# Integer softmax of a vision tower: the left-over part is made by GpSimd in three passes

## The reference

```python
def _int_exp(x_int, s, n=30):
    x0_int = jnp.floor(LN2 / s)
    x_int = jnp.maximum(x_int, n * x0_int)
    q = ste_floor(x_int / x0_int)
    r = x_int - x0_int * q
    exp_int, es = _int_polynomial(r, s)
    exp_int = jnp.maximum(ste_floor(exp_int * jnp.exp2(n - q)), 0.0)
    return (exp_int, es / 2.0 ** n)
```

## Time and profile before

| | us |
|---|---|
| median of 3 runs | 561.8 |
| lowest and highest run | 560.23, 562.18 |
| the profiled execution, whole | 560.4 |
| its span in the profile | 558.6 |
| busy in the span: TensorE | 419.3 |
| VectorE | 317.6 |
| ScalarE | 247.1 |
| GpSimd | 143.7 |

### The profile page before, as it was taken

How to read it: one execution, slowest core, us unless ns; L and a number is a source line. 1 busy time by engine, 2 the same in 40 slices (tenths; PEclk the granted TensorE clock), 3 DMA queues, 4 the chain that set the end, 5 groups by cost and what they waited for, 6 DMA issues and landing times.

```text
span 558.6 us, 9536 instructions
## 1 busy us (share of the span) xinstructions
PE 419.3 (75%) x3508; PEld 308.4 (55%) x3509; DVE 317.6 (57%) x867; ACT 247.1 (44%) x518; POOL 143.7 (26%) x169
## 2 busy tenths in 40 slices
PE   4777785468778999999889994632794235799997
PEld 3545562246568885666555793321442233589996
DVE  3858875489855421223311128669898975645642
ACT  4235543336656411222222212693396665385661
POOL 3644443069911240000000054008010001113410
PEclk9969987559999999999999998575556555599999
DMA  8921111096004222111101071000000000000002
GB/s 296 404 105 19 17 18 19 14 397 284 4 1 193 84 101 86 48 47 39 58 19 39 29 287 51 0 1 3 2 0 0 2 5 1 2 0 1 1 19 72
DMA packets 19793, 38.64 MB, mean 69 GB/s; under 512 B 2136, under 2 KB 16164, under 8 KB 18340
## 3 DMA queue, kind: packets, MB, share of 16 engines
q1 hardware_dynamic: 18788, 35.41, 18.3%
q0 software_dynamic: 960, 2.62, 1.4%
HBM read 29.77 MB, written 7.01 MB: 66 GB/s over the span
## 4 chain that ended last, share of the span: by engine, by line
PE 52%; DVE 24%; ACT 10%; issue 6%; POOL 6%; DMA 1%; SPq 0%; DVEq 0%; ACTq 0%
PE psum L1255 11%; PE psum L1262 6%; PE psum L1287 5%; PE psum L2337 4%; PE psum L1301 3%; PE psum L2370 3%; POOL ring L782 3%; POOL experts L787 2%; PE psum L610 2%; PE psum L2376 2%; PE psum L1279 1%; ACT experts L1663 1%; PE psum L2354 1%; DMA experts<-in_tern 1%; DVE ring L1939 1%
## 5 line engine op out<-in xcount | busy, mean ns | idle before, releaser
L1255 PE MATMUL psum<-experts,ring 128*128 x136 | 64.3, 596 | 1.9 <-issue 1.2
L1079 DVE TENSOR_TENSOR ring<-ring,psum 128x512 f32<-128x512 f32 x17 | 11.7, 688 | 62.8 <-PE psum L1255 62.8
L1186 POOL DMA_INDIRECT front<-expert_results,slot_of x10 | 9.9, 992 | 125.0 <-DMA expert_results<-ring 122.2
L1262 PE MATMUL psum<-front,shared 128*128 128x256 f32 (+1 forms) x160 | 34.6, 370 | 0.0
L1255 PEld LDWEIGHTS psum<-experts,ring 128*128 128x128 f32 x136 | 23.3, 190 | 19.4 <-issue 19.4
L1287 PE MATMUL psum<-experts,ring 128*128 x136 | 32.1, 379 | 0.0
L1287 PEld LDWEIGHTS psum<-experts,ring 128*128 128x128 f32 x136 | 25.8, 190 | 10.3 <-issue 7.6
L1262 PEld LDWEIGHTS psum<-front,shared 128*128 128x128 f32 x160 | 29.2, 190 | 3.2
L1385 ACT COPY ring<-psum 128x512 f32<-128x512 f32 x17 | 10.0, 586 | 42.3 <-PE psum L1279 42.3
L2337 PE MATMUL psum<-experts 128*128 128x256 f32 (+1 forms) x120 | 28.6, 384 | 0.0
L590 PE MATMUL psum<-experts,ring 128*128 128x256 f32 x108 | 25.9, 391 | 0.4 <-DVE experts L485 0.4
(11 more groups left out here) (364 smaller groups left out, 1076.0 us busy)
## 6 DMA issues: line engine op xcount, KB each, us to landing
experts<-in_experts SPq DMA_DIRECT2D x8, 1536.0 KB, 12.8
experts<-in_x SPq DMA_DIRECT2D x9, 384.0 KB, 8.2
expert_rows<-zeros SPq DMA_DIRECT2D x1, 2176.0 KB, 15.0
ring<-expert_rows SPq DMA_DIRECT2D x17, 128.0 KB, 2.1
shared<-in_shared SPq DMA_DIRECT2D x1, 1536.0 KB, 18.1
experts<-in_ffn_q SPq DMA_DIRECT2D x1, 1536.0 KB
experts<-in_ffn_s SPq DMA_DIRECT2D x1, 1536.0 KB
experts<-in_pos_embed SPq DMA_DIRECT2D x1, 1152.0 KB, 8.7
```

Of the source, the lines that this page charges most:

```text
L1079: nc.vector.tensor_tensor(o, o, up_bank(g), ALU.mult).then_inc(hidden_done.sem, 1)
L1255: mm = nc.tensor.matmul(bank, sl_xT[t % 2][:, k, :], slot_w(t, block, k, F), start=(k == 0), stop=(k == KD - 1))
L1262: mm = nc.tensor.matmul(o[:, b, 0:w], shared_w(block, k, (2 * half + b) * P, P), moe_x(c)[:, k, 0:w], start=(k == 0), stop=(k == KD - 1))
```

## The change

The pass left_over leaves VectorE. GpSimd does it in three passes: it copies `sm_d` to a new f32 buffer `sm_f` (two buffers, behind the others in `ring`), multiplies `sm_v` by minus x0 into `sm_r`, waits for that through a new semaphore count `sm_scaled`, and adds `sm_f`. The waits of left_over on exponential(t-3), whole(t) and shifted(t) go with it, and so does the signal `sm_left`, which ScalarE's whole and squared and VectorE's shifted wait for. The two memsets stand behind GpSimd's tile 4 instead of behind `k_root`, and clear only the half of each region that the V copies don't write.

```diff
+        sm_f = [view(ring, 4352 + u * N1, N1) for u in range(2)]
...
+        sm_scaled = Count("sm_scaled", pool_power, TOK)
...
-            def left_over(t):
-                dve.wait_ge(sm_whole.sem, sm_whole.done(t))
-                dve.wait_ge(sm_shifted.sem, sm_shifted.done(t))
-                if t >= 3:
-                    dve.wait_ge(sm_exp.sem, sm_exp.done(t - 3))
-                nc.vector.scalar_tensor_tensor(sm_r[t % 3], sm_v[t % 2], x0_neg, sm_d[t % 3], ALU.mult, ALU.add).then_inc(sm_left.sem, 1)
-
...
-                if 0 <= i - 1 < NT:
-                    left_over(i - 1)
...
-            pool.wait_ge(pv_vb_ready.sem, pv_vb_ready.done(0))
-            nc.gpsimd.memset(l1_f[:, 1, :], 0.0)
-            nc.gpsimd.memset(l1_f[:, 4, :], 0.0).then_inc(pv_zeroed.sem, 1)
+
+            def left_over(t):
+
+                pool.wait_ge(sm_shifted.sem, sm_shifted.done(t))
+                nc.gpsimd.tensor_scalar(sm_f[t % 2], sm_d[t % 3], 1.0, None, ALU.mult)
+                pool.wait_ge(sm_whole.sem, sm_whole.done(t))
+                if t >= 3:
+                    pool.wait_ge(sm_exp.sem, sm_exp.done(t - 3))
+                nc.gpsimd.tensor_scalar(sm_r[t % 3], sm_v[t % 2], x0_neg, None, ALU.mult).then_inc(sm_scaled.sem, 1)
+                pool.wait_ge(sm_scaled.sem, sm_scaled.done(t))
+                nc.gpsimd.tensor_tensor(sm_r[t % 3], sm_r[t % 3], sm_f[t % 2], ALU.add).then_inc(sm_left.sem, 1)
+
+            for t in range(NT):
+                left_over(t)
+                if t == 4:
+                    pool.wait_ge(pv_vb_ready.sem, pv_vb_ready.done(0))
+                    for a, i in enumerate((1, 4)):
+                        w = nc.gpsimd.memset(l1_f[:, i, :].rearrange("p (g a d) -> p g a d", a=2, d=HD // 2)[:, :, 1 - a, :], 0.0)
+                    w.then_inc(pv_zeroed.sem, 1)
```

## The result

The changed kernel takes 579.8 us (median of 4 runs, 577.3 to 581.3), the kernel before beside it 561.7; the ratio is 1.035, 95% interval 1.031 to 1.040. The medians lie 18.1 us apart, and the ratio stands for 19.9, where 8.0 were forecast; 577.5 was the top of the range. The span of the profiled execution is 578.2 us, against 558.6.

What follows compares the result with a forecast made beforehand. Before, ScalarE's order ends the softmax stage; after, GpSimd with the port (3.38 us a tile against ScalarE's 2.75) starts the last square 8.2 us later, taken as 8.0: 561.8 + 8.0 = 569.8 us, range 565.0 to 577.5.

Steps and rivals of the forecast that it cites:

- What is added on GpSimd: Integer softmax, per tile: two tensor_scalars at 0.60 + 0.62 us, 0.08 wait and 1.24 add, 2.54 us undisturbed.
- The upper bound I gave: Most that each new GpSimd tensor_scalar was taken to cost: the price of the add, 1.27 us each.
- The exclusion: Two-input VectorE passes and GpSimd instructions reading SBUF exclude each other; each blocked softmax pass costs GpSimd 0.46 us.
- the term of 0.92 us a tile: GpSimd's waits behind VectorE's shifted pass and exponential, 0.46 us each, within the 3.38 us tile.
- the term of the passes: GpSimd's copy and scaling tensor_scalars in each softmax tile, taken as 0.60 + 0.62 us.
- the add's own wait: GpSimd's add waits 0.08 us for the scaling; with the port, this was to lie under VectorE's exponential.
- No gain from VectorE: Ten L1824 passes leaving VectorE free 6.6 us, costed at no gain: ScalarE's order and TensorE's LoRA end hide it.
- (a): Rival: no exclusion of these softmax passes, GpSimd tile 2.54 us, 562.3 us, no change; chance 0.13.
- (b): Rival: whole instructions exclude each other, no start hidden; 4.04 us a tile, 6.1 us more, 575.9; chance 0.12.
- (c): Rival: int16 read or SBUF factor makes GpSimd tensor_scalars dearer, up to 1.27 us: 582.8, one only 576; chance 0.10.
- (d): Rival: faster, VectorE's 6.6 us count after all, needing ScalarE's last whole pass before 423.56; chance 0.03.
- The rest only shifts: Behind the last square the same instructions follow at the same clock, so later stages keep their length, only later.

## Why the prediction was wrong

**The bound was right, its price was not.** GpSimd became the bound of the stage, with the direction and the place that were forecast. The step that failed is in "What is added on GpSimd": "I take 0.60 + 0.62". The term measured 1.47 + 1.57, counted from start to start (the second is 1.65 less the 0.08 of the add's own wait). Of the two differences that I named (int16, a factor from SBUF) the first costs nothing and the second 0.07 us; the one that counts I did not see, though it stands in the code behind the row: L2242 has two operations (`1.0 / 7.5, -1.0, ALU.mult, ALU.add`), the new passes one. The upper bound I gave, the add's 1.27, was too low as well: it was chosen as a row of the same engine, not as the most that the form could cost.

**The exclusion.** Its price for fast instructions was right: 0.42 and 0.48 us against 0.46 once the passes have two operations, and the sum made with it, 8.0 us, is met by the kernel that it describes, 7.6 us. In the change as it is, it hardly appears: the slow passes held VectorE's for 0.35 us and were not held themselves. So the term of 0.92 us a tile was too high by all of it, while the term of the passes was too low by 1.8 us, and the add's own wait, which was to lie under the exponential, cost its 0.08: a tile cost 4.34 us and not 3.38. Seven such tiles make 6.7 us; tile 0 took 4.4 us instead of 3.0, tiles 8 and 9 together 8.8 instead of 5.5. These 11.4 us, less 0.2 for the V rounding and the memsets, are the 11.2 between the stage forecast (8.2 longer) and measured (19.4).
The Trainium skill's page "SBUF — State Buffer", section "Who interferes with whom", has the exclusion last for the whole instruction. The adds agree with it but for the first 0.14 us; the slow tensor_scalars, 1.49 us long, held a two-input pass for 0.35 us, so for them the runs disagree; the V rounding's 1.76 us fit a hold to the end of one.

**No gain from VectorE.** Right, and shown by taking the ten passes out.

**Rivals.** (a), no exclusion, has its wait-free GpSimd rows, but is refuted by the idle adds and by the kernel with two operations. (b), nothing of a start hidden, is not borne out: there a tile cost 3.50 us and not 4.04. (c) had the right term, dearer tensor_scalars, but neither cause nor size: it allowed up to 0.65 us more a pass, and 0.9 came. Its dear end, 582.8, lies near the 579.8 measured by luck, since the exclusion that it kept in the sum fell away; I gave (c) 0.10 and left this end outside the range. (d) is refuted by the run without the left-over.

**The rest only shifts.** Nearly. From `k_root` the difference is 19.4 us at the last square, and 19.6 - 1.64 = 17.96 us at the end of the span. Of the 1.4 us between the two, 1.1 are the first stretch of the FFN. Busy time and granted clock (the third number from the end, as a share of full speed) from the last power of the output stage to the FFN's first, before and after:

```profile
484.70:490.10 5.40, 5.40 (x28) 4.51 (x27) 2.05 (x6) 3.28 (x10) 0.69 (x1) 0.85 0.00 2
```

```profile
505.40:509.70 4.30, 4.30 (x27) 3.67 (x26) 1.90 (x6) 3.30 (x10) 0.80 (x1) 1.00 0.00 0
```

The granted clock was 0.85 there in one and 1.00 in the other. In the other traces of this study the stretch took 3.7 to 5.3 us, whatever the kernel, so this is not put down to the change.

## What to carry to other kernels

Price an instruction by a row of its own form, down to the number of its operations, and where no row has it, let the upper bound be wide or measure it alone: here a missing "plus 0.0" in two instructions was worth 10.5 us of the stage. Before work is moved off a busy engine, ask which engine's order ends the stage; a run with the work taken out altogether tests it, and here it gained nothing. An engine that stands idle beside VectorE is not free for reads: the fast GpSimd instructions of these runs that read SBUF had to be paid together with the VectorE passes of two inputs beside them, 0.42 to 0.48 us for each.

## What the runs showed of the hardware

- On GpSimd a tensor_scalar with one operation took 1.50 us for 128 x 512, the same with two 0.62, a copy 0.61 (f32 and int16), the factor from SBUF 0.07 more.
- Beside a 1.5 us tensor_scalar of that slow form a two-input VectorE pass took at most 1.1 us, beside a 1.26 us add 1.75 us; the row sums, with one input, took 0.67 us beside either. The V rounding, with one input too, took 1.76 us for 1.49 when it began in the last 0.4 us of a slow instruction.
- Twelve GpSimd adds with no reader made the softmax 8.6 us longer.
